# Half of the weight-tile loads moved from the sync queue to the scalar queue, in an 8-core mLSTM and 4-bit-FFN kernel

## The chip, the cores and the metric

The kernel runs on the 8 cores of one Trainium2 chip. Each core computes one of the eight sequences of the batch with a full copy of the weights; the cores exchange nothing. The time is that of the slowest core, in microseconds (us) of one execution.

## The reference

```python
# x: (8, 2048, 2048) float32; one (2048, 2048) sequence per core
x = x + _L0_attn_ref(_layernorm(x), ...)   # mLSTM attention, out projection, gated MLP (FF = 8192)
x = x + _L0_ffn_ref(_layernorm(x), ...)

def _L0_ffn_ref(x1, w_up_q, w_up_scale, b_up, w_up_lora_a, w_up_lora_b,
                w_down_q, w_down_scale, b_down, w_down_lora_a, w_down_lora_b):
    def dequant4bit(q, scale):             # q is int32 holding 0..15, one scale for 64 columns
        return (q.astype(jnp.float32) - 7.5) * jnp.repeat(scale, 64, axis=1)
    w_up = dequant4bit(w_up_q, w_up_scale).T          # w_up_q  (8192, 2048)
    y1 = x1 @ w_up + b_up + x1 @ w_up_lora_a @ w_up_lora_b
    x2 = jax.nn.relu(y1)
    w_down = dequant4bit(w_down_q, w_down_scale).T    # w_down_q (2048, 8192)
    return x2 @ w_down + b_down + x2 @ w_down_lora_a @ w_down_lora_b
```

## The kernel before

A small builder class, `Bld`, keeps one list of instructions for each of the five engines (sync, gpsimd, scalar, vector, tensor). Whatever is appended to a list is executed on that engine in exactly that order: `b.do` appends an operation, `b.wait` a wait on another engine's counter, `b.wait_tok` a wait for a DMA's semaphore, and `b.dma(q, ...)` the issue of a DMA by engine `q`. So a DMA that is appended to the scalar list stands behind every activation, and every wait of an activation, that was appended before it. The program text itself is the schedule; no planner reorders it.

Stages, in order: layernorm and projections; the mLSTM heads; output gate and out projection (these end at about 2880 us of the span). Then the three stages that matter here.

**Dequantisation** (`dq_tile`, L993 to L1035, and the loops L1037 to L1061). It runs once per core and writes both 4-bit weights, transposed and in bfloat16, to the DRAM scratch tensors `scr_wup` and `scr_wdn`. `dq_tile` handles one tile: a load into one of two buffers `qtile[slot]` (L999; the slot is the parity of a running tile number, and the load waits for the dequantisation of the tile two before); one vector operation that dequantises it into `dqt` (L1006); then, in groups of four, 128x128 transposes on TensorE into one of two PSUM tiles `ps_tq` (L1020), each group copied by the scalar engine into a stage buffer (L1029). For the up weight a tile is 128x2048 int32 (1 MB, four groups), and after every 4 tiles the stage buffer (2 MB) is written out by sync (L1045): 16 such rounds. For the down weight a tile is 128x4096 (2 MB, eight groups), and after every 4 tiles 4 MB are written (L1059): 8 rounds. Before each write sync waits for the last copy of the round, and after it the scalar list has a wait for the write's landing, ahead of the next round's copies. Below, the four tiles of a round are called A, B, C and D; A and C are in slot 0, B and D in slot 1.

**The gated MLP** (`d_group`, twice) does not touch the changed lines.

**The 4-bit FFN** (`e_group`, four times, 512 rows each). Its up half (from L1470) runs over 64 column blocks `oc`. Each block is 16 matmuls (L1497) and one rank-16 matmul with the small tile `lub` (L1502), into one of two PSUM tiles `ps_y1`, followed by one Relu activation on the scalar engine (L1509) that writes `u2T`. Four blocks share one weight buffer `wupt[fb % 2]` of 2 MB, where `fb = oc // 4`; its load (L1479) is appended at the first of the four blocks, before that block's matmuls and after the Relu of the block before, and waits until the matmuls of `fb - 2` have read the buffer. The tile `lub` (4 KB) is loaded by gpsimd (L1486) two blocks ahead. Afterwards a rank-16 product `ps_l` is formed (L1517), and the down half (L1566) takes `u2T` and `scr_wdn`, whose tiles `wdt` (512 KB) the scalar queue already loads (L1556), with nothing else on the scalar engine in that half, and with `ycl` loaded by sync (L1547).

Of the kernel before, what the change touches and what calls it, by code (L numbers as in the profile page):

```python
# [144 lines left out]
def build_core(taps=()):  # L145
# [39 lines left out]
    b = Bld(nc)  # L185
    es = contextlib.ExitStack()
    with es:
        b.alloc_sems(es)

        def sb(name, shape, dtype, stack=es):  # L190
            return stack.enter_context(nc.sbuf_tensor(name, shape, dtype))

        def ps(name, shape, dtype, stack):
            return stack.enter_context(nc.psum_tensor(name, shape, dtype))
# [331 lines left out]
        with contextlib.ExitStack() as pb:  # L526
# [7 lines left out]
            with contextlib.ExitStack() as pbp:  # L534
# [4 lines left out]
                for idx, (wname, off) in enumerate([("wk", KOFF), ("wq", QOFF)]):  # L539
                    for oc in range(8):  # L540
                        gi = idx * 8 + oc
                        slot = gi % 2
# [72 lines left out]
        with contextlib.ExitStack() as pm:  # L615
# [18 lines left out]
            with contextlib.ExitStack() as pmp:  # L634
# [13 lines left out]
                for h in range(H):  # L648
                    slot = h % 2
# [121 lines left out]
        with contextlib.ExitStack() as pc:  # L771
# [19 lines left out]
            with contextlib.ExitStack() as pcp:  # L791
# [20 lines left out]
                for st in range(4):  # L812
# [3 lines left out]
                    for oc in range(NCH):  # L816
                        gi = st * NCH + oc
                        slot = gi % 2
# [34 lines left out]
                    for hh in range(H):  # L853
# [42 lines left out]
                        for k in range(2):  # L896
                            r = 2 * hh + k
                            if st > 0 or hh > 0 or k > 0:
# [4 lines left out]
                                scalar=mhw_pp[:, r:r + 1],  # L903
# [67 lines left out]
        with contextlib.ExitStack() as pq:  # L971
            sup_sb = sb("sup_sb", [128, 64 * 32], F32, pq)
            sdn_sb = sb("sdn_sb", [128, 16 * 128], F32, pq)
            qtile = [sb("qt0", [128, 4096], I32, pq), sb("qt1", [128, 4096], I32, pq)]
            dq_t = [sb("dqt0", [128, 4096], BF16, pq), sb("dqt1", [128, 4096], BF16, pq)]
            stageU = sb("stageU", [128, NCH * 512], BF16, pq)
            stageD = sb("stageD", [128, 32 * 512], BF16, pq)
            tok_q = [b.dsem(es), b.dsem(es)]
            tok_sc = b.dsem(es)
            tok_stg = b.dsem(es)  # L980
            b.dma("sync", tok_sc, lambda e: e.dma_start(
                out=sup_sb[:].rearrange("p (fb c) -> p fb c", c=32),
                in_=I["s_up"].rearrange("(fb p) c -> p fb c", p=128)))
            b.dma("sync", tok_sc, lambda e: e.dma_start(
                out=sdn_sb[:].rearrange("p (db c) -> p db c", c=128),
                in_=I["s_dn"].rearrange("(db p) c -> p db c", p=128)))
            b.wait_tok("vector", tok_sc)
            with contextlib.ExitStack() as pqp:
                ps_t = [ps("ps_tq0", [128, 512], BF16, pqp), ps("ps_tq1", [128, 512], BF16, pqp)]
                state = {"seq": 0, "pkey": {0: None, 1: None}, "tpk": {0: None, 1: None},  # L990
                         "v_dq": {}, "t_tp": {}, "s_ev": {}}

                def dq_tile(qsrc, rows, cols, srep, stage, woff, nch_t):  # L993
                    st8 = state
                    slot = st8["seq"] % 2
                    width = cols[1] - cols[0]
                    if st8["pkey"][slot] is not None:
                        b.wait("sync", "vector", st8["v_dq"][st8["pkey"][slot]])
                    lq = b.dma("sync", tok_q[slot], lambda e, qsrc=qsrc, rows=rows, cols=cols, slot=slot, width=width: e.dma_start(  # L999
                        out=qtile[slot][:, 0:width],  # L1000
                        in_=qsrc[rows[0]:rows[1], cols[0]:cols[1]]))
                    b.wait_tok("vector", tok_q[slot], lq)
                    if st8["pkey"][slot] is not None:
                        b.wait("vector", "tensor", st8["t_tp"][st8["pkey"][slot]])
                    key = st8["seq"]
                    st8["v_dq"][key] = b.do("vector", lambda e, slot=slot, srep=srep, width=width: e.scalar_tensor_tensor(  # L1006
                        out=dq_t[slot][:, 0:width].rearrange("p (c r) -> p c r", r=64),
                        in0=qtile[slot][:, 0:width].rearrange("p (c r) -> p c r", r=64),
                        scalar=7.5, in1=srep,
                        op0=ALU.subtract, op1=ALU.mult))  # L1010
                    st8["pkey"][slot] = key
                    b.wait("tensor", "vector", st8["v_dq"][key])
                    for g4 in range(nch_t // 4):
                        pbk = g4 % 2
                        if st8["tpk"][pbk] is not None:
                            b.wait("tensor", "scalar", st8["s_ev"][st8["tpk"][pbk]])
                        tm = 0
                        for jj in range(4):
                            c = g4 * 4 + jj
                            fn = lambda e, slot=slot, c=c, pbk=pbk, jj=jj: e.transpose(  # L1020
                                ps_t[pbk][:, jj * 128:(jj + 1) * 128],
                                dq_t[slot][:, c * 128:(c + 1) * 128], identb[:])
                            if jj == 3:
                                tm = b.do("tensor", fn)
                            else:
                                b.do_("tensor", fn)
                        st8["t_tp"][key] = tm
                        b.wait("scalar", "tensor", tm)
                        sev = b.do("scalar", lambda e, g4=g4, woff=woff, stage=stage, pbk=pbk: e.activation(  # L1029
                            out=stage[:].rearrange("p (c f) -> p c f", f=512)[  # L1030
                                :, g4 * 4:(g4 + 1) * 4, woff:woff + 128],
                            in_=ps_t[pbk][:].rearrange("p (c f) -> p c f", f=128),
                            func=AF.Identity))
                        st8["s_ev"][(key, g4)] = sev
                        st8["tpk"][pbk] = (key, g4)  # L1035
                    st8["seq"] += 1

                for fbg in range(16):
                    for fbi in range(4):
                        fb = fbg * 4 + fbi  # L1040
                        srep = sup_sb[:, fb * 32:(fb + 1) * 32].unsqueeze(2).broadcast_to([128, 32, 64])
                        dq_tile(I["q_up"], (fb * 128, (fb + 1) * 128), (0, 2048), srep,
                                stageU, fbi * 128, 16)
                    b.wait("sync", "scalar", b.cnt["scalar"])
                    b.dma("sync", tok_stg, lambda e, fbg=fbg: e.dma_start(  # L1045
                        out=scr_wup[fbg].rearrange("c p f -> p c f"),
                        in_=stageU[:].rearrange("p (c f) -> p c f", f=512)))
                    b.wait_tok("scalar", tok_stg)
                for dbg in range(4):
                    for fh in range(2):  # L1050
                        for dbi in range(4):
                            db = dbg * 4 + dbi
                            srep = sdn_sb[:, db * 128 + fh * 64: db * 128 + fh * 64 + 64
                                          ].unsqueeze(2).broadcast_to([128, 64, 64])
                            dq_tile(I["q_dn"], (db * 128, (db + 1) * 128),
                                    (fh * 4096, (fh + 1) * 4096), srep,
                                    stageD, dbi * 128, 32)
                        b.wait("sync", "scalar", b.cnt["scalar"])
                        b.dma("sync", tok_stg, lambda e, dbg=dbg, fh=fh: e.dma_start(  # L1059
                            out=scr_wdn[dbg, fh * 32:(fh + 1) * 32].rearrange("j p d -> p j d"),  # L1060
                            in_=stageD[:].rearrange("p (j d) -> p j d", d=512)))  # L1061
                        b.wait_tok("scalar", tok_stg)
            b.barrier()
# [234 lines left out]
        with contextlib.ExitStack() as pe:  # L1298
# [12 lines left out]
            tok_wupt = [b.dsem(es), b.dsem(es)]  # L1311
# [32 lines left out]
            def e_group(ge):  # L1344
# [5 lines left out]
                with contextlib.ExitStack() as peu:  # L1350
# [7 lines left out]
                    with contextlib.ExitStack() as pep:  # L1358
# [10 lines left out]
                        for mi in range(4):  # L1369
                            rge = ge * 4 + mi  # L1370
                            slot = mi % 2
# [42 lines left out]
                        for mi in range(4):  # L1414
                            rge = ge * 4 + mi
                            slot = mi % 2
# [52 lines left out]
                        t_fb_use = {}  # L1469
                        t_oc = {}  # L1470
                        s_relu = {}
                        lwu = 0
                        for oc in range(64):
                            fb = oc // 4
                            wslot = fb % 2
                            if oc % 4 == 0:
                                if fb > 1:
                                    b.wait("sync", "tensor", t_fb_use[fb - 2])
                                lwu = b.dma("sync", tok_wupt[wslot], lambda e, fb=fb, wslot=wslot: e.dma_start(  # L1479
                                    out=wupt[wslot][:].rearrange("p (c f) -> p c f", f=512),  # L1480
                                    in_=scr_wup[fb].rearrange("c p f -> p c f")))
                            slot = oc % 2
# [48 lines left out]
                with contextlib.ExitStack() as ped:  # L1531
# [6 lines left out]
                    with contextlib.ExitStack() as peq:  # L1538
# [4 lines left out]
                        for nt in range(4):  # L1543
                            slot = nt % 2
# [154 lines left out]
```

How the kernel before makes its waits and increments, by code:

```python
        def thunk(eng, fn=fn, sem=tok[0], tgt=tok[1]):  # L58
            fn(eng).then_inc(sem, 16)
# [5 lines left out]
    def wait_tok(self, e, tok, val=None):  # L65
        if val is None:
            val = tok[1]
        if val <= 0:
            return
        self.ops[e].append(
            lambda eng, sem=tok[0], val=val: eng.wait_ge(sem, val))
# [5 lines left out]
        def thunk(eng, fn=fn, e=e, step=step):  # L77
            fn(eng).then_inc(self.sems[e], step)
# [9 lines left out]
    def wait(self, e, other, val):  # L88
        if val <= 0:
            return
        self.ops[e].append(
            lambda eng, other=other, val=val: eng.wait_ge(self.sems[other], val)
        )
        self.tail_inc[e] = False
# [7 lines left out]
            def thunk(eng, e=e):  # L102
                eng.nop().then_inc(self.sems[e + "_m"], 1)
# [15 lines left out]
    def barrier(self):  # L119
        self.s_settle()
        for tok in getattr(self, "all_toks", []):
            if tok[1] > 0:
                self.wait_tok("sync", tok)
                self.wait_tok("gpsimd", tok)
        marks = {e: self.mark(e) for e in ENGS}
        for e in ENGS:
            for o in ENGS:
                if o != e:
                    sem = o + "_m" if o in ("sync", "gpsimd") else o
                    self.ops[e].append(
                        lambda eng, sem=sem, val=marks[o]: eng.wait_ge(self.sems[sem], val))
```

## Time and profile before

| | us |
|---|---|
| median of 2 runs | 9420.49 (9418.9 to 9422.09) |
| the profiled execution | 9409.62 |
| its span, slowest core (core 4) | 9408.1 |
| spans of the eight cores | 9282.6 to 9408.1 |
| dequantisation, up weight | 2880 to 3354 |
| dequantisation, down weight | 3354 to 3768 |
| up half of the 4-bit FFN, four times | 294.3, 289.4, 291.1, 294.7 |

A row of the page's groups gives the line, the engine, the tile written and those read, the count, the busy time and the mean duration of one, and then the idle time of the engine just before these instructions and what ended most of it. The chain of waits follows the work that ended last back from the end; a DMA entry in it is time in which everything downstream waited for that transfer to land. In a timeline a row is start, duration, engine, line, operation and tiles, with the idle time before it in brackets. SPq and ACTq are the DMA-issuing sequencers of sync and scalar.

### The profile page before, as it was taken

How to read it: one execution, taken by the hardware profiler on the slowest of the kernel's cores; microseconds unless marked ns; L12 is line 12 of the kernel's file. 1: busy time of each engine (PE TensorE's matmuls, PEld its weight loads, DVE VectorE, ACT ScalarE, POOL GpSimd, SP SyncE). 2: the span in 40 equal slices, each digit the busy share in tenths (PEclk: the TensorE clock that was granted, in tenths of full speed). 3: DMA queues.
4: the chain of work that ended last, by engine and by line, in shares of the span. 5: the costliest groups of instructions: out<-in, count | busy, mean ns of one | idle time of the engine just before them, and what ended most of it. 6: DMA issues, size and time to landing. Idle time of an engine off the chain costs nothing.

```text
span 9408.1 us, 77707 instructions; the slowest of 8 cores (9282.6 to 9408.1 us)
## 1 busy us (share of the span) xinstructions
PE 6875.3 (73%) x29728; PEld 2920.6 (31%) x29728; DVE 1663.5 (18%) x2310; ACT 1151.6 (12%) x1793; POOL 695.2 (7%) x875
## 2 busy tenths in 40 slices
PE   1698666655553233699988699998778688688688
PEld 0233111122212122344433244443333233233233
DVE  3211444222222333100000200000100100100100
ACT  1000333210012233100000100000010010010110
POOL 0000000000000000111100011110210010000000
PEclk9877777777776555799999799999889899899899
DMA  4231000366656677688855588865543434434434
GB/s 144 55 44 37 27 10 10 45 89 86 84 69 190 212 244 241 92 77 76 77 100 108 88 76 76 76 84 107 97 131 117 152 117 126 143 99 148 139 112 140
DMA packets 1286646, 974.84 MB, mean 104 GB/s; under 512 B 744779, under 2 KB 1230284, under 8 KB 1263612
## 3 DMA queue, kind: packets, MB, share of 16 engines
q0 software_dynamic: 829312, 295.20, 29.4%
q1 hardware_dynamic: 321814, 540.44, 17.1%
q10 hardware_dynamic: 135168, 134.23, 4.8%
q8 instruction: 254, 4.16, 0.2%
q14 instruction: 98, 0.80, 0.0%
HBM read 1138.95 MB, written 125.96 MB: 134 GB/s over the span
## 4 chain that ended last, share of the span: by engine, by line
PE 63%; DMA 18%; DVE 10%; issue 4%; ACT 3%; SPq 1%; DVEq 0%; ACTq 0%; POOLq 0%; POOL 0%
PE ps_e L1566 10%; PE ps_d L1264 8%; PE ps_y1b L1497 5%; PE ps_ga L1196 5%; PE ps_ub L1202 5%; PE ps_gb L1196 5%; PE ps_ua L1202 5%; DMA lub<-lub 3%; DMA qt<-q_up 3%; PE ps_b L593 3%; PE ps_b L557 3%; DMA wog<-wog 3%; PE ps_y1a L1497 3%; DMA qt<-q_dn 2%; PE ps_o L831 2%
## 5 line engine op out<-in xcount | busy, mean ns | idle before, releaser
L1566 PE MATMUL ps_e<-wdt,u2T 128*128 128x512 bf16 x4096 | 926.3, 391 | 107.7 <-DVE outst L1594 72.7
L1264 PE MATMUL ps_d<-wd,uT 128*128 128x512 bf16 x4096 | 915.0, 386 | 115.4 <-DVE ystage L1283 70.6
L1020 PE MATMUL ps_tq<-identb,dqt 128*128 128x128 bf16 x2048 | 271.4, 302 | 616.8 <-DVE dqt L1006 540.5
L1566 PEld LDWEIGHTS ps_e<-wdt,u2T 128*128 128x128 bf16 x4096 | 409.0, 100 | 625.0 <-issue 168.7
L1264 PEld LDWEIGHTS ps_d<-wd,uT 128*128 128x128 bf16 x4096 | 404.0, 99 | 626.4 <-issue 167.5
L831 PE MATMUL ps_o<-hintile,wog 128*128 128x512 bf16 x1024 | 289.0, 451 | 185.2 <-DMA wog<-wog 184.9
L1020 PEld LDWEIGHTS ps_tq<-identb,dqt 128*128 128x128 bf16 x2048 | 183.2, 130 | 705.2 <-issue 679.8
L697 ACT ACTIVATE E_sb<-M_rep,Gcol 128x512 f32<-128x512 f32 x320 | 224.4, 717 | 993.7 <-DVE M_rep L671 739.5
L593 PE MATMUL ps_b<-wv_ct,big_a 128*128 128x512 bf16 x1024 | 270.0, 437 | 61.0 <-DMA wv_ct<-wv 60.1
L1497 PE MATMUL ps_y1b<-x1pT,wuptb 128*128 128x512 bf16 x1024 | 252.7, 404 | 66.2 <-DMA lub<-lub 64.4
L1497 PE MATMUL ps_y1b<-x1pT,wupta 128*128 128x512 bf16 x1024 | 250.2, 401 | 59.2 <-DMA lub<-lub 59.2
L1486 POOL DMA_DIRECT2D lub<-lub x256 | 124.9, 491 | 2141.2 <-PE ps_y1a L1502 634.3
L557 PE MATMUL ps_b<-big_a,wkq 128*128 128x512 bf16 x1024 | 263.6, 430 | 9.4 <-DMA wkq<-wk 9.4
L939 PE MATMUL ps_x<-wout_nt,houtT 128*128 128x512 bf16 x1024 | 235.3, 394 | 17.1 <-DMA wout_nt<-wout 15.2
L710 DVE TENSOR_TENSOR C_sb<-ps_qk,E_sb 128x512 bf16<-128x512 f32 x320 | 218.9, 690 | 138.1 <-PE ps_qk L683 116.8
L1196 PE MATMUL ps_ga<-h2T,wg_cba 128*128 128x512 bf16 x1024 | 234.8, 383 | 3.4 <-DVE h2T L1165 1.4
L1497 PE MATMUL ps_y1a<-x1pT,wupta 128*128 128x512 bf16 x1024 | 232.0, 379 | 5.2 <-DVE tupT L1468 3.7
L1196 PE MATMUL ps_ga<-h2T,wg_cbb 128*128 128x512 bf16 x1024 | 231.4, 379 | 5.8 <-DMA wu_cbb<-wup 2.7
L1215 DVE TENSOR_TENSOR uT<-sil,ps_ua 128x512 bf16<-128x512 bf16 x128 | 88.1, 688 | 816.0 <-ACT sil L1212 816.0
L1497 PE MATMUL ps_y1a<-x1pT,wuptb 128*128 128x512 bf16 x1024 | 232.1, 380 | 0.2 <-issue 0.2
L1202 PE MATMUL ps_ub<-h2T,wu_cbb 128*128 128x512 bf16 x1024 | 231.5, 379 | 0.0
L1196 PE MATMUL ps_gb<-h2T,wg_cba 128*128 128x512 bf16 x1024 | 231.5, 379 | 0.0
(199 smaller groups left out, 6843.3 us busy)
## 6 DMA issues: line engine op xcount, KB each, us to landing
wdt<-scr_wdn ACTq DMA_DIRECT2D x256, 512.0 KB, 4.0
qt<-q_up SPq DMA_DIRECT2D x64, 1024.0 KB, 9.4
qt<-q_dn SPq DMA_DIRECT2D x32, 2048.0 KB, 12.6
wd<-wdown POOLq DMA_DIRECT2D x128, 512.0 KB, 5.5
wupta<-scr_wup SPq DMA_DIRECT2D x32, 2048.0 KB, 7.9
wuptb<-scr_wup SPq DMA_DIRECT2D x32, 2048.0 KB, 8.0
xbuf<-x SPq DMA_DIRECT2D x32, 1024.0 KB, 8.3
wog<-wog POOLq DMA_DIRECT2D x64, 512.0 KB, 8.3
```

What stands on the lines that cost most here:

```text
L557: fn = lambda e, slot=slot, c=c, pbk=pbk, nt=nt: e.matmul(ps_b[pbk][:], wkq_cb[slot][:, c * 128:(c + 1) * 128], hinT[:, c * S + nt * 512: ...
L593: fn = lambda e, c=c, m=m, pbk=pbk: e.matmul(ps_b[pbk][:], hinT[:, c * S + m * 128: c * S + (m + 1) * 128], wv_ct[:, c * 512:(c + 1) * 512 ...
L697: sE = b.do("scalar", lambda e, h=h, st=st, tc=tc, qx=qx: e.activation(out=E_sb[qx][:], in_=M_rep[:, st * 512:(st + 1) * 512], func=AF.Exp ...
L710: vC[ti] = b.do("vector", lambda e, qx=qx: e.tensor_mul(C_sb[qx][:], ps_qk[qx][:], E_sb[qx][:]))
L831: fn = lambda e, slot=slot, gi=gi, c=c: e.matmul(ps_o[gi % 4][:], wog_cb[slot][:, c * 128:(c + 1) * 128], hintile[:, c * 512:(c + 1) * 512 ...
L939: fn = lambda e, c=c, mi=mi, sx=sx, wsl=wsl: e.matmul(ps_x1[sx][:], houtT[:, c * 512 + mi * 128: c * 512 + mi * 128 + 128], wout_nt[wsl][: ...
L1020: fn = lambda e, slot=slot, c=c, pbk=pbk, jj=jj: e.transpose(ps_t[pbk][:, jj * 128:(jj + 1) * 128], dq_t[slot][:, c * 128:(c + 1) * 128], ...
L1196: b.do_("tensor", lambda e, c=c, s2=s2, gx=gx, ws=ws: e.matmul(ps_g[gx][:], wg_cb[ws][:, c * 128:(c + 1) * 128], h2T[:, c * 1024 + s2 * 51 ...
L1202: fn = lambda e, c=c, s2=s2, gx=gx, ws=ws: e.matmul(ps_u[gx][:], wu_cb[ws][:, c * 128:(c + 1) * 128], h2T[:, c * 1024 + s2 * 512: c * 1024 ...
L1264: fn = lambda e, j=j, jj=jj, mi=mi, js=js: e.matmul(ps_d[mi][:], uT[:, j * 1024 + mi * 128: j * 1024 + (mi + 1) * 128], wd_t[js][:, jj * 5 ...
L1497: b.do_("tensor", lambda e, c=c, oc=oc, slot=slot, wslot=wslot: e.matmul(ps_y1[slot][:], wupt[wslot][:, c * 512 + (oc % 4) * 128: c * 512 ...
L1566: fn = lambda e, j=j, jj=jj, mi=mi, js=js: e.matmul(ps_d[mi][:], u2T[:, j * 512 + mi * 128: j * 512 + (mi + 1) * 128], wdn_t[js][:, jj * 5 ...
```

## The change

Of the loads into double-buffered tiles, those of slot 0 stay on the sync queue and those of slot 1 go to the scalar queue, in two places: the quantised tiles in `dq_tile`, and the up-weight blocks `wupt` in `e_group`. The wait ahead of each moved load moves with it. Their places in the program text stay as they are. No operation, size or buffer changes.

```diff
                 def dq_tile(qsrc, rows, cols, srep, stage, woff, nch_t):
                     st8 = state
                     slot = st8["seq"] % 2
+                    qq = "sync" if slot == 0 else "scalar"
                     width = cols[1] - cols[0]
                     if st8["pkey"][slot] is not None:
-                        b.wait("sync", "vector", st8["v_dq"][st8["pkey"][slot]])
-                    lq = b.dma("sync", tok_q[slot], lambda e, ...: e.dma_start(
+                        b.wait(qq, "vector", st8["v_dq"][st8["pkey"][slot]])
+                    lq = b.dma(qq, tok_q[slot], lambda e, ...: e.dma_start(
...
                             if oc % 4 == 0:
+                                wq = "sync" if wslot == 0 else "scalar"
                                 if fb > 1:
-                                    b.wait("sync", "tensor", t_fb_use[fb - 2])
-                                lwu = b.dma("sync", tok_wupt[wslot], lambda e, ...: e.dma_start(
+                                    b.wait(wq, "tensor", t_fb_use[fb - 2])
+                                lwu = b.dma(wq, tok_wupt[wslot], lambda e, ...: e.dma_start(
```

## Rows read from the trace of the kernel before

**Rows 1.** The page: the chain of waits by line, share of the span.
```profile
PE ps_e L1566 10%; PE ps_d L1264 8%; PE ps_y1b L1497 5%; PE ps_ga L1196 5%; PE ps_ub L1202 5%; PE ps_gb L1196 5%; PE ps_ua L1202 5%; DMA lub<-lub 3%; DMA qt<-q_up 3%; PE ps_b L593 3%; PE ps_b L557 3%; DMA wog<-wog 3%; PE ps_y1a L1497 3%; DMA qt<-q_dn 2%; PE ps_o L831 2%
```
**Rows 2.** Timeline of one up round: tiles A, B, C, and the write.
```profile
3037.81 4.72 DVE L1006 SCALAR_TENSOR_TENSOR dqt<-qt,sup_sb 128x2048 bf16<-128x2048 int32 x2 [16.91 <-DMA qt<-q_up]
...
3042.55 1.09 ACT L1029 ACTIVATE stageU<-ps_tq 128x512 bf16<-128x512 bf16 x2 [0.34 <-PE ps_tq L1020]
...
3045.15 2.29 DVE L1006 SCALAR_TENSOR_TENSOR dqt<-qt,sup_sb 128x2048 bf16<-128x2048 int32 x1 [2.61 <-DMA qt<-q_up]
3045.40 1.08 ACT L1029 ACTIVATE stageU<-ps_tq 128x512 bf16<-128x512 bf16 x2 [0.34 <-PE ps_tq L1020]
...
3053.80 0.38 SPq L1045 DMA_DIRECT2D scr_wup<-stageU  x1
```
**Rows 3.** The chain of waits in order of time, up rounds: start, us, what.
```profile
3040.18 4.81 DMA qt<-q_up
...
3220.00 8.30 DMA qt<-q_up
```
**Rows 4.** Timeline of one down round: tile A, last copies of A and B, write.
```profile
3518.99 4.43 DVE L1006 SCALAR_TENSOR_TENSOR dqt<-qt,sdn_sb 128x4096 bf16<-128x4096 int32 x1 [24.25 <-DMA qt<-q_dn]
...
3528.62 1.08 ACT L1029 ACTIVATE stageD<-ps_tq 128x512 bf16<-128x512 bf16 x2 [0.34 <-PE ps_tq L1020]
...
3534.75 1.09 ACT L1029 ACTIVATE stageD<-ps_tq 128x512 bf16<-128x512 bf16 x2 [0.34 <-PE ps_tq L1020]
...
3551.93 0.38 SPq L1059 DMA_DIRECT2D scr_wdn<-stageD  x1
```
**Rows 5.** The chain of waits in the same down round.
```profile
3501.56 7.23 SPq L999
3508.88 16.08 DMA qt<-q_dn
...
3529.62 11.36 DMA qt<-q_dn
```
**Rows 6.** DMA view, 3523 to 3541 us: issues, KB each, median us to landing.
```profile
qt<-q_dn SPq DMA_DIRECT2D x2, 2048.0 KB, 11.2
```
**Rows 7.** Timeline in the FFN's up half, at the change from fb 0 to fb 1.
```profile
6879.09 0.39 PE L1502 MATMUL ps_y1b<-tupT,lub 16*128 16x512 bf16 x1
...
6879.40 3.63 PE L1497 MATMUL ps_y1a<-x1pT,wuptb 128*128 128x512 bf16 x16
6879.55 0.36 SPq L1479 DMA_DIRECT2D wupta<-scr_wup  x1
6879.57 0.69 ACT L1509 ACTIVATE u2T<-ps_y1b,bup_pp 128x512 bf16<-128x512 f32 x1 [3.19 <-PE ps_y1b L1502]
...
6886.91 6.13 PE L1497 MATMUL ps_y1b<-x1pT,wuptb 128*128 128x512 bf16 x16 [3.56 <-DMA lub<-lub]
```
**Rows 8.** Waits in the first up half (engine, line, waited for: total us, times, longest).
```profile
PE ps_y1b L1497 <- DMA lub<-lub: 33.9, 15, 3.6
```
**Rows 9.** The page's DMA issues: KB each, median us to landing.
```profile
wdt<-scr_wdn ACTq DMA_DIRECT2D x256, 512.0 KB, 4.0
...
wuptb<-scr_wup SPq DMA_DIRECT2D x32, 2048.0 KB, 8.0
```
**Rows 10.** DMA view, 7172 to 7186 us: GB/s in 40 slices, and both hardware queues.
```profile
GB/s 0 0 0 0 0 6 76 0 135 413 366 392 363 372 401 404 339 339 342 360 395 404 401 407 386 415 392 404 407 389 383 386 389 386 380 179 76 0 0 0
...
q1 hardware_dynamic: 1056, 2.10, 44.0%
q10 hardware_dynamic: 1584, 1.57, 32.3%
```
**Rows 11.** Windows before and after that stop: us, busy times, PEclk, DMA share, GB/s.
```profile
6864.00:6879.00 15.00, 15.00 (x67) 6.10 (x66) 0.00 (x0) 2.06 (x3) 1.46 (x3) 1.00 0.02 2
6887.00:6892.00 5.00, 5.00 (x13) 1.69 (x13) 0.00 (x0) 0.00 (x0) 0.00 (x0) 0.50 0.33 113
```
**Rows 12.** Windows of the four up halves: the sum of their lengths and busy times.
```profile
sum 1169.50, PE 1036.11 PEld 413.53 DVE 0.00 ACT 178.07 POOL 120.16; mean PE 259.03 PEld 103.38 DVE 0.00 ACT 44.52 POOL 30.04
```

More of the change, by code:

```diff
@@ L995, in dq_tile @@
                     slot = st8["seq"] % 2
+                    qq = "sync" if slot == 0 else "scalar"
                     width = cols[1] - cols[0]
                     if st8["pkey"][slot] is not None:
-                        b.wait("sync", "vector", st8["v_dq"][st8["pkey"][slot]])
-                    lq = b.dma("sync", tok_q[slot], lambda e, qsrc=qsrc, rows=rows, cols=cols, slot=slot, width=width: e.dma_start(
+                        b.wait(qq, "vector", st8["v_dq"][st8["pkey"][slot]])
+                    lq = b.dma(qq, tok_q[slot], lambda e, qsrc=qsrc, rows=rows, cols=cols, slot=slot, width=width: e.dma_start(
                         out=qtile[slot][:, 0:width],
@@ L1476, in e_group @@
                             if oc % 4 == 0:
+                                wq = "sync" if wslot == 0 else "scalar"
                                 if fb > 1:
-                                    b.wait("sync", "tensor", t_fb_use[fb - 2])
-                                lwu = b.dma("sync", tok_wupt[wslot], lambda e, fb=fb, wslot=wslot: e.dma_start(
+                                    b.wait(wq, "tensor", t_fb_use[fb - 2])
+                                lwu = b.dma(wq, tok_wupt[wslot], lambda e, fb=fb, wslot=wslot: e.dma_start(
                                     out=wupt[wslot][:].rearrange("p (c f) -> p c f", f=512),
```

## The prediction

> **What bounds the kernel now.** I read the page first, then the chain of waits, then timelines of the two places that the diff touches. Its largest entries are matmuls; among the transfers are qt, at 3% for the up and 2% for the down weight, and lub at 3% [rows 1]. So both places are on the path today, and any stretch added to either comes out at the end, unless something else there shrinks.
>
> In the dequantisation each round is a chain, not a full engine. In an up round DVE stands 16.91 us for tile A's load, dequantises A and B back to back, waits 2.61 us for C, and the write goes out 15.99 us after A's start [rows 2]. The loads of B and D are ready or nearly so when DVE wants them, because sync, which has nothing else to do, issues each as soon as its buffer is free. A down round is the same with larger tiles, 32.94 us from A's start to the write [rows 4]. In the FFN's up half a block takes 3.88 us (one Relu of 0.69 and 3.19 idle before the next) and TensorE stops only for lub, once per weight block: 3.56 us at the first [rows 7], 33.9 us over 15 stops in the first pass [rows 8]. That stop comes when a 2 MB weight load has been issued just ahead of the lub load. The weight itself is never waited for: it takes 8.0 us [rows 9] and is issued four blocks (15.5 us) ahead.
>
> **What the change does to the order.** No work is added or removed. What moves is 32+16 issues of qt and 32 of wuptb, each with its wait, past everything on the scalar list. The wait itself costs nothing there: it is always already met. What costs is what stands ahead of the load. For tile B these are the stage copies of A; for D, those of C; for an odd fb, the Relu of the block just before. These copies need A's transposes, and the Relu needs the last matmul before the one that wants the weight. So the moved loads can't be early any more. Behind each load on the scalar engine stand only copies or Relus that need that load's data anyway; sync loses half of its issues and keeps its waits. The issue itself is short: 0.36 us on sync [rows 7].
>
> **Up rounds (16).** T is the start of A's dequantisation, 3037.81. Today the write follows at T+15.99. A's last copy ends at 3042.55+1.09, T+5.83 [rows 2]. New: B's load is issued at T+5.95. C's was issued by sync at T+2.4, so B and C share the engines, just as C and D do today; the entry for such a load is 4.81 us, and 8.30 in one round [rows 3]; I take 5.2 for B, near the commoner. DVE starts B at T+11.3, and C behind it. B's copies end 5.83 later (T+17.1), C's 2.84 after those (as B's behind A's today: 3046.48 against 3043.64 [rows 2]), T+19.95. D's load is issued at T+20.1, alone, 5.0 us (by the same row), DVE at T+25.25, last copy T+31.1, write T+31.25. That is +15.3 a round, 16 rounds: **+244 us**. Does A land sooner, now that B's load no longer queues with it? In the down round A's data is in use at 3518.99 and B's has landed 16.08 us after 3508.88, so 6 us later [rows 4, 5]: the two came one after the other, so A gains nothing. The bound on the other side is a full share, 1 MB at 390 GB/s, 2.7 us a round (43 us) and double that in a down round (43 us).
>
> **Down rounds (8).** T is 3518.99; today the write is at T+32.94 (3551.93). A's last copy ends at 3528.62+1.08, T+10.71 [rows 4]. B's load is issued at T+10.85, 6.4 us after C's. Today's D is issued 6.1 us after C and lands in 11.36 us [rows 5]; the same for B: DVE at T+22.4. B's copies end at T+33.1. C's follow: today's B ends its copies 6.1 us after A (3535.84 against 3529.70), T+39.2. D issued T+39.35. Alone, such a load takes about 11.1 us (C today is alone for its first 6 us; the median of the two is 11.2 [rows 6]); the lower bound is 8.0, the 2 MB of wuptb [rows 9], or 25 us less over 8 rounds. DVE at T+50.6, last copy T+61.3, write T+61.45: +28.5 a round, **+228 us**.
>
> **FFN up half (4 times).** At the start of an odd fb the last matmul of the even one ends at 6879.48 (6879.09+0.39); sync issues the next even load 0.07 us later, the Relu ends at 6880.26, and only then the scalar queue issues the load that TensorE needs at once [rows 7]. So 4 MB are in flight together, in 7 of the 8 odd fb (with the last, nothing is left for sync to load). How fast are two hardware queues together? Where both are loaded, the rate is 340 to 415 GB/s, about 385 in the mean [rows 10]. 4.19 MB at 385 GB/s is 10.9 us; the fixed part is 8.0 [rows 9] less 5.5 us (2.1 MB at that rate), 2.4. Stop: 0.07+2.4+10.9 = 13.4 us. Alone: 0.8 to the issue and 8.0, 8.8 us. That is also the lower bound for all eight. I take 13.4, since the rows with both queues are this case; for the upper end I take the poorer rate of the down-weight loads, 4.2 MB in the 17.5 us from C's issue to D's landing [rows 4, 5].
>
> After a stop the clock is low: granted 0.50 (1.2 GHz) from 6887 to 6892, where it was 1.00 (2.4 GHz) before the 3.56 us stop [rows 11]. The 16 matmuls take 6.13 instead of 3.63 us [rows 7]: 2.5 us for each stop. So a pass gains stops of 7x13.4+8.8+8x2.5 = 122.6 us.
>
> Something goes in exchange. The lub stops happen because a weight load is issued just before; now every weight load starts and ends inside a stop, and the lub load with it. A pass of 64 blocks at 3.88 is 248.3 us, plus 1.4 us for the last Relu and the operation behind it (0.69 each, an estimate from the Relu's row [rows 7]); the four passes take 1169.5 us, 292.4 each [rows 12], so 42.7 us a pass are lub stops with their cold restarts, and I take them all as gone. Net 79.9 a pass, **+320 us**. If none goes, it is 171 us more.
>
> **Sum.** 244+228+320 = 792 us on the profiled 9409.6 is 10,202; the median of the runs is 11 above that execution: **10,210 us**, +8.4%.
>
> **Rivals.**
>
> *The two queues don't slow each other.* Then every FFN stop is 8.8 us: 28x4.6 = 129 us less; if A also lands sooner, another 86 and D's 25: between 9,970 and 10,080. For it: the 512 KB loads on the scalar queue take 4.0 us at the median with little beside them [rows 9]. Against: both together reach no more than about 400 GB/s [rows 10]. Chance 0.14.
>
> *The pairs collide harder.* If the FFN's pair needs 17.5 us, 28x4.1 = 115 more; B as slow as the slowest such entry, 8.30 [rows 3], 50 more; half of the lub stops left, 85 more: 10,330 to 10,460. For it: eight cores now ask for 4 MB at a time. Against: they aren't in step, and their spans already differ by 125 us. Chance 0.11.
>
> *The loads stay early and only the issue time is saved.* The mechanism would be that the scalar sequencer runs ahead of its activations' waits and issues B and the odd weights as soon as the buffer is free. Then nothing is exposed, and sync no longer sits 7.23 us on a full queue in each down round [rows 5]; if that were all on the path, 8x7.23 = 58 us less: 9,360, within 2%. It decides only if a load can pass a Relu whose wait isn't met; the Relus start 0.09 us after their matmuls in strict turn [rows 7], which speaks against it. Chance 0.03. The Trainium skill (DMA: Bandwidth & Descriptors, "Issuing engines are not separate DMA queues") states this rule: all issuers feed the same 16 DMA engines, and more issuers save only the time of issuing. By that rule alone the change would be worth at most those 58 us; the trace agrees with its first half (no more than 415 GB/s [rows 10]), and the order on the scalar list is what it leaves out.
>
> *Two queues really move more.* DVE's and TensorE's waits would shrink; a fifth off the 5% of the span that the chain has in qt [rows 1] would be 94 us, with the 171 us of lub stops gone too it would be 9,420-265 = 9,155. It needs early issue as well, and a rate above today's. Chance 0.01.
>
> **How the numbers follow.** The forecast has 0.70, with its own range 10,120 to 10,300. Leaving out the far ends of the second and third case gives 10,020 to 10,350. Within 2% is about what the measurement can't tell from no change: slower by more has 0.95, within 2% has 0.03 (the third rival), faster 0.02 (the fourth, and 0.01 for what no row shows).
>
> **What would show it.** After: up rounds of 44 to 45 us and down rounds of 79; two long DVE waits on qt more in each round; TensorE waiting on wupt about 13 us, 7 times a pass, and 9 us once; hardly a lub stop; up halves of about 372 us. The forecast is wrong if the scalar queue's loads are issued before the copies ahead of them have ended, if wupt stops are near 9 us or the rounds grow by less than 10 and 20 us, or if another stage moves by more than 20 us.

## The result, and the profile after

The changed kernel takes 10,005 us in the median of its undisturbed executions (9,996 to 10,104), the kernel before 9,363 us in the same series (9,337 to 9,422): ratio **1.071 (95% interval 1.065 to 1.076)**, some 650 us slower. The profiled execution is 10,091 us. A part of all executions had a lower granted clock on one die; every number here is from executions, or dies, without that. The forecast was 10,210 us, with a range of 10,020 to 10,350. The profiled execution lies in it, and so does the ratio on the 9,420 us that the forecast started from (10,086); the series' own median, 10,005, is 15 us below its lower end, with the kernel before at 9,363 us here.

| stage, us | before, 8 cores | after, 8 cores | difference | forecast |
|---|---|---|---|---|
| dequantisation, up | 461 to 475 | 639 to 664 | +180 | +244 |
| dequantisation, down, to the MLP's first load | 414 to 421 | 569 to 575 | +155 | +228 |
| gated MLP | 3003 to 3025 | 3011 to 3024 | 0 | 0 |
| 4-bit FFN | 2603 to 2633, one pair 2675 | 2946 to 2948 on four cores, 3005 to 3067 on the others | +330 on the four | +320 |
| sum of the stages | | | +665 | +792 |

A stage runs from its first load to that of the next one; the last begins with the loads of `ybk`. Differences are between means: up and down over all cores, the FFN over the six cores before and the four after that are near each other.

The page of the changed kernel (core 3, the slowest), its chain of waits by line, shows the moved loads where rows 1 had lub; qt is 6% where it was 5%.

```profile
span 10089.5 us, 77707 instructions; the slowest of 8 cores (9996.1 to 10089.5 us)
PE ps_e L1568 10%; PE ps_d L1265 8%; PE ps_y1a L1499 5%; PE ps_y1b L1499 5%; PE ps_ga L1197 4%; PE ps_ub L1203 4%; PE ps_ua L1203 4%; PE ps_gb L1197 4%; DMA wuptb<-scr_wup 4%; DMA qt<-q_up 3%; DMA qt<-q_dn 3%; DMA wog<-wog 2%; PE ps_b L593 2%; PE ps_b L557 2%; DVE dqt L1007 2%
```

The waits of the changed kernel (engine, line, waited for: total us, times, longest). DVE's two waits on qt were 322.7 and 251.9 us before (core 4), and no wait on a wupt load stood in that list.

```profile
DVE dqt L1007 <- DMA qt<-q_up: 510.9, 48, 21.5
PE ps_y1a L1499 <- DMA wuptb<-scr_wup: 420.2, 32, 14.1
DVE dqt L1007 <- DMA qt<-q_dn: 418.1, 24, 24.6
```

The 48 and 24 waits are three for each of the 16 and 8 rounds: A, B and D. The timeline of one up round after (tiles A, B and C, D, write), to be read beside [rows 2]:

```profile
3160.54 0.38 SPq L1046 DMA_DIRECT2D scr_wup<-stageU  x1
...
3170.91 2.29 DVE L1007 SCALAR_TENSOR_TENSOR dqt<-qt,sup_sb 128x2048 bf16<-128x2048 int32 x1 [13.91 <-DMA qt<-q_up]
...
3175.56 1.08 ACT L1030 ACTIVATE stageU<-ps_tq 128x512 bf16<-128x512 bf16 x2 [0.34 <-PE ps_tq L1021]
3176.12 0.33 ACTq L1000 DMA_DIRECT2D qt<-q_up  x1
3181.15 4.49 DVE L1007 SCALAR_TENSOR_TENSOR dqt<-qt,sup_sb 128x2048 bf16<-128x2048 int32 x2 [7.95 <-DMA qt<-q_up]
3189.20 0.33 ACTq L1000 DMA_DIRECT2D qt<-q_up  x1
3193.97 2.29 DVE L1007 SCALAR_TENSOR_TENSOR dqt<-qt,sup_sb 128x2048 bf16<-128x2048 int32 x1 [8.33 <-DMA qt<-q_up]
3199.78 0.38 SPq L1046 DMA_DIRECT2D scr_wup<-stageU  x1
```

The scalar queue issues B's load at 3176.12, behind A's last copies, and D's at 3189.20. DVE stands 7.95 and 8.33 us for them, and the round is 39.24 us long. One detail is new: B's load goes out just after the last of A's copies has started (3175.56 begins two of them, which end at 3176.64), not when it has ended.

The FFN after, at the change from an even to an odd weight block, the counterpart of [rows 7]:

```profile
7162.55 0.39 PE L1504 MATMUL ps_y1b<-tupT,lub 16*128 16x512 bf16 x1
7163.01 0.36 SPq L1481 DMA_DIRECT2D wupta<-scr_wup  x1
7163.03 0.69 ACT L1511 ACTIVATE u2T<-ps_y1b,bup_pp 128x512 bf16<-128x512 f32 x1 [3.19 <-PE ps_y1b L1504]
7163.10 0.40 ACTq L1481 DMA_DIRECT2D wuptb<-scr_wup  x1
...
7176.66 5.65 PE L1499 MATMUL ps_y1a<-x1pT,wuptb 128*128 128x512 bf16 x16 [13.72 <-DMA wuptb<-scr_wup]
```

TensorE stands 13.72 us, because two loads of 2 MB leave 0.09 us apart. The chain of waits in the first pass has seven such entries and one shorter one, the last, where sync has nothing more to load:

```profile
7116.25 13.32 DMA wuptb<-scr_wup
7163.10 13.20 DMA wuptb<-scr_wup
...
7402.12 13.26 DMA wuptb<-scr_wup
7449.19 7.83 DMA wuptb<-scr_wup
```

### The profile page after: what moved, and what is told of

It reads as the page before. It is cut to its first block, busy times and chain, and to the rows that moved or that the text cites. A ratio compares the mean times of both kernels' runs of the same rounds, so it can differ in the third digit from the quotient of the medians.

```text
span 10089.5 us, 77707 instructions; the slowest of 8 cores (9996.1 to 10089.5 us)
## 1 busy us (share of the span) xinstructions
PE 6936.0 (69%) x29728; PEld 2934.1 (29%) x29728; DVE 1661.3 (16%) x2310; ACT 1150.0 (11%) x1793; POOL 695.2 (7%) x875
## 4 chain that ended last, share of the span: by engine, by line
PE 62%; DMA 19%; DVE 10%; issue 4%; ACT 3%; SPq 1%; DVEq 0%; ACTq 0%; POOL 0%; POOLq 0%
PE ps_e L1568 10%; PE ps_d L1265 8%; PE ps_y1a L1499 5%; PE ps_y1b L1499 5%; PE ps_ga L1197 4%; PE ps_ub L1203 4%; PE ps_ua L1203 4%; PE ps_gb L1197 4%; DMA wuptb<-scr_wup 4%; DMA qt<-q_up 3%; DMA qt<-q_dn 3%; DMA wog<-wog 2%; PE ps_b L593 2%; PE ps_b L557 2%; DVE dqt L1007 2%
## 5 line engine op out<-in xcount | busy, mean ns | idle before, releaser
L1568 PE MATMUL ps_e<-wdt,u2T 128*128 128x512 bf16 x4096 | 995.3, 411 | 108.8 <-DVE outst L1596 72.7
L1499 PE MATMUL ps_y1a<-x1pT,wuptb 128*128 128x512 bf16 x1024 | 310.8, 471 | 422.6 <-DMA wuptb<-scr_wup 420.2
L1499 PEld LDWEIGHTS ps_y1a<-x1pT,wuptb 128*128 128x128 bf16 x1024 | 113.7, 116 | 605.0 <-issue 555.5
L593 PE MATMUL ps_b<-wv_ct,big_a 128*128 128x512 bf16 x1024 | 229.2, 388 | 61.6 <-DMA wv_ct<-wv 60.7
L939 PE MATMUL ps_x<-wout_nt,houtT 128*128 128x512 bf16 x1024 | 236.5, 395 | 18.6 <-DMA wout_nt<-wout 18.5
L1203 PE MATMUL ps_ub<-h2T,wu_cba 128*128 128x512 bf16 x1024 | 231.5, 379 | 0.0
L1203 PE MATMUL ps_ua<-h2T,wu_cbb 128*128 128x512 bf16 x1024 | 231.5, 379 | 0.0
## 6 DMA issues: line engine op xcount, KB each, us to landing
wupta<-scr_wup SPq DMA_DIRECT2D x32, 2048.0 KB, 11.8
wuptb<-scr_wup ACTq DMA_DIRECT2D x32, 2048.0 KB, 13.3
```

The source lines that it names most:

```text
L593: fn = lambda e, c=c, m=m, pbk=pbk: e.matmul(ps_b[pbk][:], hinT[:, c * S + m * 128: c * S + (m + 1) * 128], wv_ct[:, c * 512:(c + 1) * 512 ...
L939: fn = lambda e, c=c, mi=mi, sx=sx, wsl=wsl: e.matmul(ps_x1[sx][:], houtT[:, c * 512 + mi * 128: c * 512 + mi * 128 + 128], wout_nt[wsl][: ...
L1203: fn = lambda e, c=c, s2=s2, gx=gx, ws=ws: e.matmul(ps_u[gx][:], wu_cb[ws][:, c * 128:(c + 1) * 128], h2T[:, c * 1024 + s2 * 512: c * 1024 ...
L1499: b.do_("tensor", lambda e, c=c, oc=oc, slot=slot, wslot=wslot: e.matmul(ps_y1[slot][:], wupt[wslot][:, c * 512 + (oc % 4) * 128: c * 512 ...
L1568: fn = lambda e, j=j, jj=jj, mi=mi, js=js: e.matmul(ps_d[mi][:], u2T[:, j * 512 + mi * 128: j * 512 + (mi + 1) * 128], wdn_t[js][:, jj * 5 ...
```

## The experiments

All share one theory: the time goes by **where in the scalar engine's list the load stands**, since it can't pass the copies and Relus ahead of it; that two loads then collide is a second cost, in the FFN. The rivals: the second queue itself costs; the two places act on each other. Ratios and whole times compare with the kernel before in the same series, stage times with its profile above.

**One place at a time: the dequantisation.** Only the first hunk of the diff.

```diff
+                    qq = "sync" if slot == 0 else "scalar"
...
-                    lq = b.dma("sync", tok_q[slot], ...
+                    lq = b.dma(qq, tok_q[slot], ...
```

> Only the qt loads of tiles B and D go to the scalar queue; the FFN is as before. Theory (the two places add up, each by the order on the scalar list): up rounds 40.4 us and down rounds 70 us as in the changed kernel, so 175+157 = about 330 us slower than before, ratio 1.035; the FFN stage unchanged. Rival (a late load in one place costs the other, by the granted clock or by the spread of the cores): well off 330 us, and another length of the FFN stage than before.

Measured: ratio 1.037 (1.032 to 1.043, from two executions of 9,653 and 9,678), 345 us on the 9,320 us of before in this series. The dequantisation takes 1227 to 1245 us on the eight cores (1208 to 1233 with the full change, 876 to 895 before); the FFN stage is as before, 2606 to 2623 us on every core. The up rounds came as expected, 629 to 664 us for 16. The down rounds took 568 us on two cores, near the 560 expected, and 589 to 605 us on six, against 569 to 575 in the changed kernel: there tile A's load lands 17.6 to 21.2 us after its issue in the mean, against 17.2 and 17.3 on the two. What chooses between these is open.

**One place at a time: the FFN.** Only the second hunk.

```diff
+                                wq = "sync" if wslot == 0 else "scalar"
...
-                                lwu = b.dma("sync", tok_wupt[wslot], ...
+                                lwu = b.dma(wq, tok_wupt[wslot], ...
```

> Only the odd wupt loads go to the scalar queue; the dequantisation is as before. Theory: seven stops of 13.7 us and one of 8.1 us in each pass, lub stops gone, so the forecast's 320 us, ratio 1.034 (up to 1.047 if the slowest core is one whose granted clock in the FFN falls, as cores 2 and 3 did in the changed kernel). Rival (the clock falls only because the dequantisation has become longer): every core's FFN stage about 330 us longer and none 440.

> The odd wupt loads on the scalar queue alone, a second profile. In the first, two cores of the eight had a FFN stage 135 us longer than the shortest at a granted clock of 0.80 against 0.85, and two more 50 us. Theory (the fall of the clock goes with the long stops, whichever cores it takes): again some pair of cores 50 us or more above the others, which stay at 2946 us. Rival (it belongs to certain cores, or was chance): the same pair, or none.

Measured: ratio 1.042 (1.029 to 1.055, from two executions of 9,661 and 9,756). The FFN stage is 2946 to 2951 us on four cores of the first profile, 2993 and 2999 on one pair, and 3071 and 3085 on another, where the granted clock of the stage is 0.80 against 0.85. The second profile has all eight cores at 2940 to 2954 us. So +330 us is what the hunk costs, and the rest came and went: in the changed kernel it sat on cores 2, 3, 6 and 7, in this run's first profile on 0, 1, 6 and 7, in its second on none, and one pair of before (6 and 7) has it too, some 60 us. So the theory that a fall of the clock belongs to the long stops didn't hold; nor did the rival, that it needs the longer dequantisation. The two hunks add up by the stages: 345+330 = 675 us, against 665 for the full change. By the whole times, 1.037 and 1.042 would make 1.079 instead of 1.071, but the second rests on two executions, and the longer of them is the one with the low clock on two pairs.

**The order without the second queue.** Everything stays on sync, but sync waits for what stood ahead of the moved loads on the scalar list.

```diff
                         b.wait("sync", "vector", st8["v_dq"][st8["pkey"][slot]])
+                    if slot == 1:
+                        b.wait("sync", "scalar", b.cnt["scalar"])
                     lq = b.dma("sync", tok_q[slot], ...
...
                                     b.wait("sync", "tensor", t_fb_use[fb - 2])
+                                if wslot == 1:
+                                    b.wait("sync", "scalar", s_relu[oc - 1])
                                 lwu = b.dma("sync", tok_wupt[wslot], ...
```

> All loads stay on the sync queue, but sync waits for the scalar engine's last appended operation ahead of B's, D's and the odd weights' load, so the order is that of the change without its second queue. Theory (order): nearly all of the dequantisation's loss returns, and a little more, since C's issue now stands behind B's: up rounds 42 to 43 us, down rounds 72 to 75, so 350 to 430 us. In the FFN the odd load is issued first and the even one behind it on the same queue, so all eight stops are near 8.1 us instead of 13.7: 4x(8x8.1+8x2.5-43) = 167 us. In all 520 to 600 us slower, ratio 1.055 to 1.064. Rival (the scalar queue itself is what costs): the time of before. Rival (the two loads share the rate whatever the queue): stops of 13.7 us here too, about 670 us slower.

Measured: ratio 1.059 (1.054 to 1.063), 547 us and inside the theory's range; the rival that the scalar queue is what costs is out. The dequantisation takes 1226 to 1238 us, as with the second queue (1227 to 1245 with the first hunk alone). Its down rounds are as expected, 72.3 to 73.1 us; its up rounds are shorter than the 42 to 43 expected, 40.4 to 40.9. The FFN stage is 2808 to 2825 us, 200 more than before and 130 less than with two queues, so the rival of 13.7 us stops is out too. Its timeline:

```profile
7167.31 0.39 PE L1506 MATMUL ps_y1b<-tupT,lub 16*128 16x512 bf16 x1
...
7168.55 0.37 SPq L1483 DMA_DIRECT2D wuptb<-scr_wup  x1
7169.01 2.22 SPq L1483 DMA_DIRECT2D wupta<-scr_wup  x1
7176.98 4.97 PE L1501 MATMUL ps_y1a<-x1pT,wuptb 128*128 128x512 bf16 x16 [9.28 <-DMA wuptb<-scr_wup]
```

Both loads are in flight here too, 0.46 us apart, but on one queue and the needed one first: it lands in 8.07 us by the chain of waits, as a lone load does, and the stop is 9.28 us. With two queues the needed one takes 13.3 us. The pages of the changed kernel and of this run have for both loads (the last number is the median from issue to landing):

```profile
wupta<-scr_wup SPq DMA_DIRECT2D x32, 2048.0 KB, 11.8
wuptb<-scr_wup ACTq DMA_DIRECT2D x32, 2048.0 KB, 13.3
...
wupta<-scr_wup SPq DMA_DIRECT2D x32, 2048.0 KB, 12.9
wuptb<-scr_wup SPq DMA_DIRECT2D x32, 2048.0 KB, 7.9
```

On two queues both land late, as loads do that share the rate all along; on one queue the first lands as if alone and the second 5 us behind it. So of the FFN's 330 us some 200 are the order and 130 are the collision of two queues. A run with two queues and the needed load issued well ahead of the other wasn't made, so how much of the 130 us hangs on the 0.09 us by which sync comes first is not shown. The expected 167 us were some 30 short, since the load waits here for the Relu's end: all 32 stops together are

```profile
PE ps_y1a L1501 <- DMA wuptb<-scr_wup: 292.7, 32, 9.8
```

that is 9.15 us each instead of 8.1.

**The second queue without the late order.** The same loads on the same queues as in the change, issued earlier on the scalar list. The edit, shortened to what it appends and where:

```diff
 # in dq_tile(k), ahead of tile k's stage copies, for odd k:
+    b.wait("scalar", "vector", v_dq[k])
+    lqs[k + 2] = b.dma("scalar", tok_q[1], <load of tile k + 2>)
 # in e_group, at the first block of an even fb:
+    b.wait("scalar", "tensor", t_fb_use[fb - 1])
+    lwus[1] = b.dma("scalar", tok_wupt[1], <load of fb + 1>)
```

> The same loads on the same two queues as in the change, but their issues stand earlier on the scalar list: B's and D's ahead of the stage copies of the tile two before, the odd weight's ahead of the Relus of the weight block before, as soon as the buffer is free. Theory (order): no stop at wupt, lub stops back, and in the dequantisation B is loaded before the write of the round before: 0 to 100 us faster than before (A no longer shares with B: 2.8 us in 16 up rounds is 45 us), ratio 0.99 to 1.00. Rival (the scalar queue or two queues at once are what costs): 300 us slower or more, ratio above 1.03.

> The hoisted loads once more, beside the three others: the first measurement, 1.0059 (0.9989 to 1.0129), leaves open whether the second queue costs anything when its loads are issued early. Theory (order alone): the same time as before, ratio 0.995 to 1.005. Rival (two queues at once cost a little even when early): 1.005 to 1.015, with the dequantisation or the up halves longer than before.

Measured: ratio 1.006 (0.999 to 1.013), above the 0.99 to 1.00 expected. The second series gave no ratio; its profile has on cores 0 to 3 spans of 9247 to 9328 us against 9283 to 9329 us before. So nearly all of the 7% comes back by moving the issues up, both queues still in use, and the rival of 300 us or more is out. The gain that I also expected, A's load without B's beside it, isn't there: on these cores the dequantisation takes 878 to 916 us, before 876 to 895; the FFN stage is 2600 to 2618 us, as before. The up rounds take 452 and 455 us on two of the four and 474 and 476 on the others (before 461 to 475), the down rounds 427 to 440 (before 415 to 420). In an up round A's load lands in 10.9 us in the mean of these cores where before has 11.3 and the run with late loads on one queue 9.5. B's load now goes out 3.4 us ahead of the write that A stands behind and runs beside it; that this is what takes A's gain away is likely, but was not tried. A cost of about 0.5% for two queues at once is neither shown nor excluded.

**The write moved instead of the loads.** Loads stay on sync. The stage writes go to the scalar queue, behind the copies that they wait for anyway, into two stage buffers.

```diff
-                    b.wait("sync", "scalar", b.cnt["scalar"])
-                    b.dma("sync", tok_stg, <write of stageU>)
-                    b.wait_tok("scalar", tok_stg)
+                    b.wait("scalar", "scalar", b.cnt["scalar"])
+                    lst[rnd] = b.dma("scalar", tok_stg[rnd % 2], <write of stg[rnd % 2]>)
...
+                    if rnd >= 2:
+                        b.wait_tok("scalar", tok_stg[rnd % 2], lst[rnd - 2])   # ahead of round rnd's copies
```

> All loads stay on sync as in the kernel before; it is the stage writes that go to the scalar queue, where they stand right behind the copies that they wait for, and there are two stage buffers, so that neither the next loads nor the next copies wait for a write. Theory (what bounds a round is which issue stands behind which, and sync's loads stand behind its write today): A's and B's loads of the next round go out as soon as their buffers are free; a round then comes near its bytes, 6.3 MB at 385 GB/s = 16.4 us up and 12.6 MB = 33 us down, against 29.5 and 50: 13x16+17x8 = up to 340 us faster, 250 if the reads run nearer 300 GB/s; ratio 0.964 to 0.973. Rival (the rate, not the order, is what holds the rounds): under 80 us faster.

Measured: no ratio; by stages on cores 0 to 3: up 332 to 337 us (461 to 475), down 324 to 336 us (414 to 421), together 661 to 670 us instead of 876 to 895, **some 220 us less**. More than the rival's 80, less than the 250 that I had as the lower end. The run changes two things at once, the queue of the writes and the second stage buffer, and how much each is worth alone was not tried. What bounds the rounds next can be read from the windows of the same stage in the combined kernel below (the last three columns are PEclk, DMA share, GB/s):

```profile
2900.00:3200.00 300.00, 118.72 (x904) 81.65 (x904) 131.84 (x51) 122.80 (x226) 0.00 (x0) 0.50 0.94 297
3200.00:3450.00 250.00, 110.14 (x824) 72.31 (x824) 110.64 (x25) 113.89 (x209) 0.00 (x0) 0.50 1.00 314
```

The DMA engines are busy for 94 to 100% of the time and move 297 to 314 GB/s; 385 GB/s, which I took from a burst of 10 us, is not held here over 250 to 300 us with reads and writes mixed.

**The small loads taken out of the FFN.**

```diff
+            b.dma("gpsimd", tok_el, lambda e: e.dma_start(out=lub_sb[:], in_=I["lub"]))
...
-                            llu = b.dma("gpsimd", tok_lub[slot], ...
-                            b.wait_tok("tensor", tok_lub[slot], llu)
```

> The kernel before, with the whole lora matrix lub (16x8192) loaded once into SBUF ahead of the four passes in place of 256 small loads. Theory (the 42.7 us a pass that the forecast called lub stops with their cold restarts): each up half 250 us instead of 292, 171 us faster, ratio 0.982. Rival (the weight load would be waited for instead, or the clock falls without such stops): less than 60 us faster.

Measured: 9,126 and 9,131 us in two executions, before 9,427 us in the one beside them and 9,302 to 9,334 in the series ahead. The FFN stage is 2433 to 2445 us on all cores, before 2603 to 2633 (one pair 2675): **some 175 us less**, as expected (171). The first up half goes from its first matmul (timeline) to the rank-16 product behind it (chain of waits):

```profile
6762.26 3.61 PE L1492 MATMUL ps_y1a<-x1pT,wupta 128*128 128x512 bf16 x16 [0.93 <-DVE tupT L1469]
...
7011.98 13.99 PE ps_l L1512 x64
```

That is 249.7 us where before had 294.3 on its slowest core. All 32 up halves of this run take 249.5 to 249.7 us; the four of before's slowest core took 292.4 in the mean, 42.7 more. So this measures the exchange term of the forecast by itself: 42.7 us a pass were lub stops.

**Both.** The writes on the scalar queue and lub loaded once.

> The stage writes on the scalar queue with two stage buffers, and lub loaded once. Theory (two separate places): the sum of the two runs beside it, 420 to 510 us faster than before, ratio 0.946 to 0.955. Rival (TensorE, busy for longer without stops, is granted a lower clock in the FFN and gives part back): ratio above 0.96, with a granted clock in the up halves under 0.96.

> The combined version once more, to get its ratio against the kernel before with an interval: 0.950 to 0.957, since its first profile shows a FFN stage 172 us and a dequantisation about 176 us shorter than in the runs beside it that lack the one or the other. Rival (the two don't add up over many runs): above 0.96.

Measured: five executions of 8,916, 8,922, 8,955, 8,990 and 9,005 us; of before, three in the same two series, 9,334, 9,422 and 9,427 us. Median against median that is 0.950, with too few of before for an interval; against the 9,302 to 9,334 us of the first series it is 0.961, just on the rivals' side of 0.96. The stages agree with the single runs: in the two profiles the dequantisation takes 669 to 685 us and the FFN 2436 to 2453 us on all eight cores, some 390 us less than before and under the 420 to 510 expected, since the writes gave less than they were to. So this is the faster kernel, by 4 to 5% against before and by some 10% against the changed one. The mechanism of the first rival, that TensorE without stops is granted a lower clock, is out: the FFN's mean granted clock is 0.91, 0.90 before, and every up half takes 249.5 to 249.7 us in the first profile, as without the moved writes.

## Why the prediction was right or wrong

The direction and the mechanism held, and the range did if the change is taken on the 9,420 us that the forecast started from; the median of the series, 10,005 us, is 15 us under it. That the profiled execution, 10,091 us, comes so near to 10,210 is in part luck: the FFN stage of its slowest core is 116 us longer than on four others, at a granted clock of 0.81 against 0.85, which nobody had forecast. Of my own signs of being wrong two came true by the letter: the scalar queue's loads are issued before the last copy ahead of them has ended, by 0.5 us, and the down rounds grew by 19.5 us, under the 20 that I had named. Point by point:

- **The order on the scalar list.** Right, and shown twice: the late order on one queue costs 547 us (5.87% of 9,320), both queues with an early order cost nothing that can be measured. The place where each load would be issued was right to within a copy: I let the load wait for the end of the last copy and of the Relu, and it is issued just after their start (7163.03 and 7163.10 in the FFN).
- **The FFN's stop.** Forecast 13.4 and once 8.8 us, measured 13.7 to 14.1 and 8.2 to 8.3 on core 3: 420.2 us over 32 stops where the forecast has 410.4 (420 to 441 on the eight cores). Right, and for the reason given: 4 MB at 385 GB/s. What the rate rows could not tell was who gets it: with one queue the needed load would have landed in 8 us.
- **The cold restart.** 5.65 us for the first 16 matmuls after a stop, 3.63 warm; the forecast had 6.13. So a restart costs 2.0 us there and not 2.5, which gives back a part of the longer stops. The granted clock after the stop:

```profile
7163.00:7176.40 13.40, 0.00 (x0) 0.00 (x0) 0.00 (x0) 0.69 (x1) 0.48 (x1) 0.66 0.92 313
7176.50:7179.00 2.50, 2.34 (x6) 0.89 (x7) 0.00 (x0) 0.00 (x0) 0.00 (x0) 0.50 0.02 7
7183.00:7207.00 24.00, 23.64 (x105) 9.66 (x104) 0.00 (x0) 4.46 (x7) 3.07 (x7) 1.00 0.02 1
```

  It is 0.50 (1.2 GHz) for the first matmuls and 1.00 (2.4 GHz) by 7183, the two levels of [rows 11].
- **The lub stops given back.** Right: the waits of `ps_y1b` on lub fall from 123.5 us to 4.6, and the run without lub loads measures the term at some 175 us against 171. I found it by asking what else the weight loads collided with; without it the FFN's term would have been 491.
- **The up rounds: mis-sized, and the step "so A gains nothing" was wrong.** Forecast +15.3 us a round; measured +11 (39.9 to 41.5 against 28.8 to 29.7). From the issues and landings of all eight cores, means over the rounds after the first:

| up round, us | before | after | forecast |
|---|---|---|---|
| A's load, issue to landing | 11.3 | 10.1 | unchanged |
| A's start to the write | 17.6 | 29.8 | 15.99, then 31.25 |
| B's issue after A's start | | 5.2 | 5.95 |

  Of the 4.3 us between, 1.2 are A's load, which lands sooner without B's beside it. I had judged the up round by the down round of core 4, where B's issue comes 7 us after A's and A gains nothing. Another 1.5 are the earlier issue of B and of D, 0.7 us each. The last 1.6 are the round that I started from: in [rows 2] the write follows A's start by 15.99 us, in the mean by 17.6, so part of what the change exposes was exposed before. The run with late loads on one queue shows that A's gain comes from B's absence and not from the second queue: A lands in 9.4 to 9.6 us there (chain of waits):

```profile
3117.13 9.40 DMA qt<-q_up
...
3157.59 9.59 DMA qt<-q_up
```

- **The down rounds: the prices of B's and D's load.** Mis-sized: 11.4 and 11.1 us in the sum, 7.35 and 7.43 in the round after:

```profile
3577.60 17.51 DMA qt<-q_dn
3605.46 7.35 DMA qt<-q_dn
3628.86 7.43 DMA qt<-q_dn
```

  So a round grew by 19.5 us and not by 28.5. The rows were those of core 4, where tile D took 11.36 us. In the same profile core 3 has 7.33 for it (chain of waits of core 3):

```profile
3353.20 7.33 DMA qt<-q_dn
```

  The eight cores of before are of two kinds, one of each in every pair of neighbours. On cores 1, 2, 4 and 6 D takes 10.4 to 12.5 us in the mean and A 17.4 to 18.5; on cores 0, 3, 5 and 7 D takes 7.4 to 8.0 and A 20.4 to 20.8. After the change all eight have 7.2 to 8.0 for B and D and 17.3 to 17.5 for A. So A gained nothing on core 4, as forecast, but some 3 us on the other kind, 2.0 in the mean of all; and its round before was as long as core 4's (20.8 and 28.9 us on core 3 add up to what 17.4 and 32.8 do on core 4). I had given 8.0 as the lower end for D alone, from the wuptb load of the same size, and should have used it for both. Why the same transfer takes 7.3 us on one core and 11.4 on another was not tried; that the neighbour reads or writes at the same time is only a guess.
- **The sum.** 792 us forecast, 665 measured; the missing 127 us are 64 in the up and 73 in the down rounds, less 10 in the FFN; the FFN with its exchange was right to 10 us. The up halves, forecast at about 372 us, take 375 to 382 on the four cores whose clock didn't fall.
- **The rule that more issuers save only issue time** (the Trainium skill, DMA: Bandwidth & Descriptors, "Issuing engines are not separate DMA queues"). The trace agrees that both queues share one rate: 4.2 MB in 13.3 us. The same page ("Queues, rings and completion order") says that a DMA engine takes turns between queues packet by packet; the runs agree, with 13.3 us for the needed load beside one on the other queue and 8.07 us ahead of one on its own. The sum has the shared rate already; what the forecast left out is that on one queue the same late order would cost 130 us less.

## What to carry to other kernels

A DMA issue is an instruction in its engine's list: before it is moved to a second queue, write down what stands ahead of it there and what that waits for. If it is the consumer's own predecessor, the prefetch is gone, whatever the queue. What is worth moving to the compute engine's queue is the transfer that has to wait for that engine anyway, here the write (some 220 us less, together with a second buffer for it). And of two loads of 2 MB issued together the one wanted sooner goes first on the same queue: there it landed in 7.9 us and the other in 12.9, on two queues they took 11.8 and 13.3. Small loads beside large ones can cost as much as either: here 256 loads of 4 KB cost some 175 us.

## What the runs showed of the hardware that was not expected

- An issue on the scalar queue that stands right behind an activation, with only a wait between that is already met, goes out 0.07 us after that activation's start, not after its end (7163.03 and 7163.10, where the Relu takes 0.69 us).
- A load of 2 MB on the scalar queue, issued 0.09 us after one of 2 MB on the sync queue, lands in 13.3 us; on the sync queue, issued 0.46 us ahead of another on the same queue, in 8.07 us.
- The granted clock of the FFN stage fell on some pairs of neighbouring cores and not on others in one and the same execution, to 0.80 to 0.83 against 0.84 and 0.85, worth 45 to 140 us of that stage. Which pair it was changed from run to run. Windows of the changed kernel from 8330 to 8380 us, in a down half, of cores 3, 5 and 1 in this order, all with TensorE busy throughout:

```profile
8330.00:8380.00 50.00, 50.00 (x192) 20.74 (x191) 0.00 (x0) 0.00 (x0) 0.00 (x0) 0.81 0.40 120
8330.00:8380.00 50.00, 50.00 (x232) 22.40 (x230) 0.00 (x0) 0.00 (x0) 0.00 (x0) 1.00 0.44 131
8330.00:8380.00 50.00, 50.00 (x226) 22.33 (x225) 0.00 (x0) 0.00 (x0) 0.00 (x0) 0.97 0.48 139
```

  Core 3 does 192 matmuls and core 5 232, a ratio of 0.83. The Trainium skill (TensorE: Matmul & The Clock Gate, "Seeing it yourself") tells of a peak-current limiter that takes a whole die to 13/16 of full speed, 0.81, once three of its cores run dense matmuls.
